# A DLRM tower on one core: the first two one-hot fields made as a couple, and the half grams of tiles 2 and 3 placed around the layers of tiles 0 to 2

## The reference, cut to what matters

```
e = stack([tbl_f[ids[:, f]] for f in 26 fields])     # (512, 26, 128)
T = concat([dense, e])                               # (512, 27, 128)
Z = einsum('bnd,bmd->bnm', T, T); z = Z[upper triangle]   # 351 numbers per sample
h = relu(concat([z, dense]) @ W_top1 + b_top1)       # 479 -> 512
h = relu(h @ W_top2 + b_top2)                        # 512 -> 256
y = h @ W_top3                                       # 256 -> 1
```

## Time and profile before

| what | value |
|---|---|
| median of 3 runs (lowest to highest) | 122.86 us (122.41 to 123.29) |
| the profiled execution's own time | 122.26 us |
| its span, first to last instruction | 120.5 us |
| TensorE busy (matmul) | 110.3 us, 92% |
| VectorE busy | 86.0 us, 71% |
| ScalarE busy | 80.3 us, 67% |
| GpSimd busy | 61.9 us, 51% |
| last one-hot matmul starts | 71.08 us |

### The profile page before, as it was taken

One profiled execution on the slowest core, in us unless ns is written; L12 is line 12 of the kernel. 1 busy time (PEld: TensorE's weight loads), 2 busy tenths in 40 slices (PEclk: granted clock), 3 DMA queues, 4 the chain that ended last, 5 costly groups with the idle time before them and its releaser, 6 DMA issues.

```text
span 120.5 us, 2624 instructions
## 1 busy us (share of the span) xinstructions
PE 110.3 (92%) x1008; PEld 92.0 (76%) x1008; DVE 86.0 (71%) x180; ACT 80.3 (67%) x150; POOL 61.9 (51%) x60
## 2 busy tenths in 40 slices
PE   5999799999999999999999975997989899859993
PEld 5967577688678888887787855996979689859990
DVE  5689999988789699787987621699722459875141
ACT  4479981977999999999976851787930029793011
POOL 7578777777777787877778674000600000022000
DMA  2999559999999269961111122000110000101000
GB/s 68 310 365 397 218 159 367 392 400 380 398 356 365 82 220 409 373 165 33 34 44 44 44 54 60 0 5 20 27 42 0 0 5 0 27 4 23 5 0 1
DMA packets 7638, 17.75 MB, mean 147 GB/s; under 512 B 1965, under 2 KB 2889, under 8 KB 7497
## 3 DMA queue, kind: packets, MB, share of 16 engines
q1 hardware_dynamic: 5770, 14.13, 31.9%
q0 software_dynamic: 1632, 3.19, 9.0%
q10 hardware_dynamic: 222, 0.26, 0.7%
HBM read 17.33 MB, written 0.00 MB: 144 GB/s over the span
## 4 chain that ended last, share of the span: by engine, by line
PE 63%; DMA 11%; DVE 9%; issue 5%; ACT 5%; SPq 5%; ACTq 0%; DVEq 0%
PE work L469 20%; PE work L471 19%; PE work L417 8%; DMA table<-small 8%; PE work L526 5%; DMA Zt<-table 4%; PE work L427 4%; SPq L328 3%; DVE hot L734 3%; PE tp L453 3%; DVE t_lo L703 2%; PE work L536 1%; DVE Zt L568 1%; ACT Zt L568 1%; ACT table L560 1%
## 5 line engine op out<-in xcount | busy, mean ns | idle before, releaser
L400 POOL DMA_INDIRECT rows<-tbl,idx x48 | 58.1, 1211 | 25.8 <-issue 12.8
L469 PE MATMUL work<-hot,t_hi 128*128 128x512 f32 x128 | 52.2, 407 | 1.1 <-DVE hot L734 0.7
L471 PE MATMUL work<-hot,t_lo 128*128 128x512 f32 x128 | 50.4, 394 | 0.0
L734 DVE TENSOR_SCALAR hot<-ids_bc,rownum 128x1024 fp32r<-128x1024 int32 (+1 forms) x59 | 38.7, 697 | 6.7 <-PE work L471 4.9
L469 PEld LDWEIGHTS work<-hot,t_hi 128*128 128x128 f32 x128 | 24.4, 190 | 10.2 <-DVE hot L734 2.5
L471 PEld LDWEIGHTS work<-hot,t_lo 128*128 128x128 f32 x128 | 24.4, 190 | 4.3
L588 ACT CAST t_hi<-table 128x1280 fp32r<-128x1280 f32 (+3 forms) x16 | 16.8, 1050 | 5.8 <-DMA table<-small 5.3
L703 DVE TENSOR_TENSOR t_lo<-table,t_hi 128x1280 fp32r<-128x1280 f32 (+3 forms) x16 | 19.5, 1220 | 1.4 <-DVE minus_row L695 1.0
L427 PE MATMUL work<-XT 128*58 128x52 f32 x512 | 15.8, 217 | 2.7 <-issue 2.1
L427 PEld LDWEIGHTS work<-XT 128*58 128x58 f32 x512 | 14.7, 133 | 4.3 <-issue 4.1
L560 ACT COPY table<-work 14x224 f32<-14x224 f32 x16 | 5.7, 355 | 13.9 <-PE work L427 13.1
(11 more groups left out here) (47 smaller groups left out, 59.2 us busy)
## 6 DMA issues: line engine op xcount, KB each, us to landing
table<-small SPq DMA_DIRECT2D x8, 640.0 KB
ids_bc<-ids_oh SPq DMA_DIRECT2D x6, 512.0 KB, 3.3
table<-small SPq DMA_DIRECT2D x4, 512.0 KB
w_sb<-w SPq DMA_DIRECT2D x1, 1024.0 KB
rows<-tbl,idx POOLq DMA_INDIRECT x48
table<-small SPq DMA_DIRECT2D x2, 320.0 KB
ids_bc<-ids_oh SPq DMA_DIRECT2D x2, 256.0 KB, 3.4
w_sb<-w SPq DMA_DIRECT2D x1, 512.0 KB
```

Source lines behind the costliest of these rows:

```text
L400: nc.gpsimd.indirect_dma_start(rows[:, t, place - FIRST, :], None, tbls[f], bass.IndirectOffsetOnAxis(ap=idx[:, t, place - FIRST:place - F ...
L469: nc.tensor.matmul(bank, t_hi[:, i % PARTS, c * D:(c + 1) * D], hot[:, k % HOTS, :], start=row_chunk(i, c) == 0, stop=False)
L471: last = nc.tensor.matmul(bank, t_lo[:, i % PARTS, c * D:(c + 1) * D], hot[:, k % HOTS, :], start=False, stop=row_chunk(i, c) == n - 1)
L734: nc.vector.tensor_scalar(hot[:, k % HOTS:k % HOTS + n, :], ids_bc[:, ids_slot(f):ids_slot(f) + n, :], rownum[:, v, at:at + 1], None, ALU. ...
```

## The change

The first two fields become a couple like the others. `SINGLES` goes; the couple's chunks alternate, and only the first chunk of each of the two fields keeps a 512-wide one-hot (`LONE = 2`); the others are 1024 wide. ScalarE makes the last couple of tables 0 and 1. The second table comes as one DMA (`HEADED = 1`), the ids of field 1 come right behind those of field 0, and the ids of fields 4 and 5 have slots of their own, so nothing waits for them. The low parts for the first two tables stand at other one-hots. The rows steps (2, 1) and (2, 2) move from the tail into the one-hot phase (after tables 11 and 12), both copied by ScalarE. In the tail `dense` of tile 0 goes first, and the halves come earlier, the layers later. The PSUM bank of each field shifts by 4, so that the bank of layer 1 is free early. Gathers 44 and 45 now wait for the fifth half, 46 and 47 for the sixth (before: 46 and 47 for the fourth).

```diff
-VECTOR_ROWS = [(2, 1), (3, 1)]
+VECTOR_ROWS = [(3, 1)]
-HEADED = 2
+HEADED = 1
-SINGLES = 2
+LONE = 2
-GATHER_AFTER = {46: ("gram", 4)}
-ACT_EVERY = 5
-ACT_TABLES = [3, 5, 6, 7, 8, 9, 10, 11, 12, 13]
+GATHER_AFTER = {44: ("gram", 5), 46: ("gram", 6)}
+ACT_TABLES = [0, 1, 3, 5, 6, 7, 8, 9, 10, 11, 12, 13]
-ROWS_AFTER = {..., 9: [(1, 2)], 11: [(2, 0)]}
+ROWS_AFTER = {..., 9: [(1, 2)], 10: [(2, 0)], 11: [(2, 1)], 12: [(2, 2)]}

-LOW_PARTS = {(i, 5 if i < SINGLES else 4 if OH_CHUNKS[i] == 8 else 6): (i + 1, 0, OH_CHUNKS[i + 1])
-             for i in range(1, K_OH - 1)}
-LOW_PARTS.update({(0, 0): (0, 0, HEAD), (0, 4): (0, HEAD, OH_CHUNKS[0]), (0, 5): (1, 0, HEAD),
-                  (1, 1): (1, HEAD, OH_CHUNKS[1])})
+LOW_PARTS = {(i, 4 if OH_CHUNKS[i] == 8 else 6): (i + 1, 0, OH_CHUNKS[i + 1]) for i in range(K_OH - 1)}
+LOW_PARTS.update({(0, 0): (0, 0, HEAD), (0, 2): (0, HEAD, OH_CHUNKS[0])})

-    steps += [("burst", 0, 0), ("gram", 0, 0), ("rows", 2, 1), ("burst", 0, 1), ("gram", 0, 1),
-              ("rows", 2, 2), ("dense", 0, 0), ("burst", 1, 0), ("gram", 1, 0), ("burst", 1, 1),
-              ("gram", 1, 1), ("layer1", 0, 0), ("layer1", 0, 1), ("rows", 3, 0), ("layer2", 0, 0), ("dense", 1, 0),
-              ("layer1", 1, 0), ("layer1", 1, 1), ("rows", 3, 1), ("layer2", 1, 0), ("burst", 2, 0), ("gram", 2, 0),
-              ("rows", 3, 2), ("burst", 2, 1), ("gram", 2, 1), ("dense", 2, 0), ("burst", 3, 0),
-              ("gram", 3, 0), ("burst", 3, 1), ("gram", 3, 1), ("layer1", 2, 0), ("layer1", 2, 1), ("dense", 3, 0),
-              ("layer2", 2, 0), ("layer1", 3, 0), ("layer2", 3, 0), ("turn", 0, 0), ("layer3", 3, 0)]
+    steps += [("dense", 0, 0), ("burst", 0, 0), ("gram", 0, 0), ("burst", 0, 1), ("gram", 0, 1), ("rows", 3, 0),
+              ("burst", 1, 0), ("gram", 1, 0), ("rows", 3, 1), ("burst", 1, 1), ("gram", 1, 1), ("burst", 2, 0),
+              ("gram", 2, 0), ("layer1", 0, 0), ("layer1", 0, 1), ("burst", 2, 1), ("gram", 2, 1), ("dense", 1, 0),
+              ("layer2", 0, 0), ("layer1", 1, 0), ("layer1", 1, 1), ("rows", 3, 2), ("burst", 3, 0), ("gram", 3, 0),
+              ("dense", 2, 0), ("layer2", 1, 0), ("burst", 3, 1), ("gram", 3, 1), ("layer1", 2, 0), ("layer1", 2, 1),
+              ("dense", 3, 0), ("layer2", 2, 0), ("layer1", 3, 0), ("layer2", 3, 0), ("turn", 0, 0), ("layer3", 3, 0)]

-    return i if i < SINGLES else i - (i - SINGLES) % 2          # pair_of
+    return i - i % 2
-    return f if f < SINGLES else (f - SINGLES + IDS - 2) % IDS  # ids_slot
+    return f % IDS
-            return work[:, (i - K_OH) % LOOKUP_BANKS, :]
+            return work[:, (i - K_OH + GRAM_BANKS) % LOOKUP_BANKS, :]

             def table_ids(i):
-                if i >= SINGLES + 2:
-                    sp.wait_ge(hot_used, groups_used(first_hot(ids_free(i))))
+                if i >= IDS:
+                    sp.wait_ge(hot_used, groups_used(first_hot(i - IDS + 2)))
-            table_ids(0)
+            for f in range(LONE):
+                sp.dma_start(ids_bc[:, f, :], ids_oh[f, :, :]).then_inc(ids_in[f], 16)

             # ScalarE, ahead of the steps and in them
             high_part(0, 0, HEAD)
+            high_part(0, HEAD, OH_CHUNKS[0])
             distance(0)
-            high_part(0, HEAD, OH_CHUNKS[0])
-            one_hot(mine_in(0)[0])
-            high_part(1, 0, HEAD)
-            distance(1)
-            high_part(1, HEAD, OH_CHUNKS[1])
+            high_part(1, 0, OH_CHUNKS[1])
...
+                    if 1 < i < K_OH - 2:
                         high_part(i + 2, 0, OH_CHUNKS[i + 2])
+                    for m in mine_in(i):
+                        one_hot(m)
+                        if i == 0:
+                            distance(1)
+                    if i <= 1:
+                        high_part(i + 2, 0, OH_CHUNKS[i + 2])
+                    if i > 1:
                         copy_lookups(i - 2)
```

More of the change, by code:

```diff
@@ L57 @@
 CHUNKS_BEHIND = 14
-GATHER_AFTER = {46: ("gram", 4)}
-ACT_EVERY = 5
-ACT_TABLES = [3, 5, 6, 7, 8, 9, 10, 11, 12, 13]
+GATHER_AFTER = {44: ("gram", 5), 46: ("gram", 6)}
+ACT_TABLES = [0, 1, 3, 5, 6, 7, 8, 9, 10, 11, 12, 13]
 DENSE_AFTER = 5
 COPIED_AFTER = 8
-ROWS_AFTER = {4: [(0, 0)], 5: [(0, 1)], 6: [(0, 2)], 7: [(1, 0)], 8: [(1, 1)], 9: [(1, 2)], 11: [(2, 0)]}
+ROWS_AFTER = {4: [(0, 0)], 5: [(0, 1)], 6: [(0, 2)], 7: [(1, 0)], 8: [(1, 1)], 9: [(1, 2)], 10: [(2, 0)], 11: [(2, 1)],
+              12: [(2, 2)]}
 GATHERED = [f for f in range(FIELDS) if f not in ONEHOT]
@@ L174, in pair_of @@
 def pair_of(i):
-    return i if i < SINGLES else i - (i - SINGLES) % 2
+    return i - i % 2
 def field_of(i, c):
-    return i if i < SINGLES else pair_of(i) + c % 2
+    return pair_of(i) + c % 2
 def row_chunk(i, c):
-    return c if i < SINGLES else (i - pair_of(i)) * OH_CHUNKS[i] // 2 + c // 2
+    return i % 2 * OH_CHUNKS[i] // 2 + c // 2
 def looked_up(f):
-    return first_hot(f + 1 if f < SINGLES else pair_of(f) + 2)
+    return first_hot(pair_of(f) + 2)
 def ids_slot(f):
-    return f if f < SINGLES else (f - SINGLES + IDS - 2) % IDS
-def ids_free(f):
-    return max(2, f - IDS + 2)
+    return f % IDS
 TABLE_OF = [i for i in range(K_OH) for _ in range(OH_CHUNKS[i])]
-HOT_FIRST = [k for k, i in enumerate(TABLE_OF) if i < SINGLES or (k - first_hot(i)) % 2 == 0]
+HOT_FIRST = [k for k in range(len(TABLE_OF)) if k < LONE or k % 2 == 0]
 def hot_width(m):
-    return 1 if TABLE_OF[HOT_FIRST[m]] < SINGLES else 2
+    return 1 if HOT_FIRST[m] < LONE else 2
 def by_scalar(m):
     i = TABLE_OF[HOT_FIRST[m]]
-    if i < SINGLES:
-        return m % ACT_EVERY == ACT_EVERY - 1
     return i in ACT_TABLES and HOT_FIRST[m] + 2 == first_hot(i + 1)
@@ L333, in table_ids @@
             def table_ids(i):
-                n = 1 if i < SINGLES else 2
-                if i >= SINGLES + 2:
-                    sp.wait_ge(hot_used, groups_used(first_hot(ids_free(i))))
-                sp.dma_start(ids_bc[:, ids_slot(i):ids_slot(i) + n, :],
-                             ids_oh[i:i + n, :, :].rearrange("f p b -> p f b")).then_inc(ids_in[i], 16)
+                if i >= IDS:
+                    sp.wait_ge(hot_used, groups_used(first_hot(i - IDS + 2)))
+                sp.dma_start(ids_bc[:, ids_slot(i):ids_slot(i) + 2, :],
+                             ids_oh[i:i + 2, :, :].rearrange("f p b -> p f b")).then_inc(ids_in[i], 16)
             sp.dma_start(idx[:], ids.rearrange("p (t f) -> p t f", t=TILES)).then_inc(idx_in, 16)
-            table_ids(0)
+            for f in range(LONE):
+                sp.dma_start(ids_bc[:, f, :], ids_oh[f, :, :]).then_inc(ids_in[f], 16)
             for i in range(K_OH):
@@ L482, in _ @@
                         pe.wait_ge(xt_ready, 1)
+                    elif halves == 1:
+                        pe.wait_ge(lookup_copied, K_OH - 1)
+                        pe.wait_ge(lookup_dve, 2)
                     if halves >= HALVES:
@@ L491, in _ @@
                     if t == 0:
-                        pe.wait_ge(lookup_copied, K_OH - 1)
-                        pe.wait_ge(lookup_dve, 2)
                         pe.wait_ge(w1_in, 16)
@@ L601, in distance @@
                 act.wait_ge(ids_in[f], 16)
+                if f == 0:
+                    act.wait_ge(ids_in[1], 16)
                 act.wait_ge(rownum_ready, 2)
@@ L633, in _ @@
             high_part(0, 0, HEAD)
+            high_part(0, HEAD, OH_CHUNKS[0])
             distance(0)
-            high_part(0, HEAD, OH_CHUNKS[0])
-            one_hot(mine_in(0)[0])
-            high_part(1, 0, HEAD)
-            distance(1)
-            high_part(1, HEAD, OH_CHUNKS[1])
+            high_part(1, 0, OH_CHUNKS[1])
             for kind, t, i in STEPS:
                 if kind == "onehot":
[L642 to L647, removed]
-                        high_part(i + 2, 0, OH_CHUNKS[i + 2])
[L649 to L654, removed]
+                    if 1 < i < K_OH - 2:
+                        high_part(i + 2, 0, OH_CHUNKS[i + 2])
+                    for m in mine_in(i):
[5 more added lines that the diff above has]
+                    if i > 1:
                         copy_lookups(i - 2)
@@ L724, in _ @@
                     dve.wait_ge(ids_in[f], 16)
-                    n = 1 if i < SINGLES else 2
-                    for c in range(0, OH_CHUNKS[i], n):
+                    for c in range(OH_CHUNKS[i]):
                         if (i, c) in LOW_PARTS and i + c:
@@ L729, in _ @@
                         k = first_hot(i) + c
[L730 to L736, removed]
+                        if k not in HOT_FIRST or by_scalar(HOT_FIRST.index(k)):
+                            continue
+                        n = hot_width(HOT_FIRST.index(k))
+                        if k == 1:
+                            dve.wait_ge(ids_in[1], 16)
+                        if k >= HOTS:
+                            dve.wait_ge(hot_used, groups_used(k + n - HOTS))
```

(12 more changed lines are left out.)

## The result

The changed kernel takes 124.96 us (median, 124.37 to 125.22) against 122.63 for the kernel before (four runs: the three of its median and one more, 120.81 to 123.29); the ratio is 1.029, 95% interval 1.025 to 1.034. It is slower, where the forecast was 122.8 us with a range up to 124.7. The profiled execution took 124.37 us, span 122.5. The ratios are of the faster runs of both kernels (they leave out nine of the 19 runs of before beside E1 to E4, more than 1.5% above the fastest), so they can differ from the quotient of the medians, which take all runs.

A forecast was written before the change was run, and what follows sets the result against it. TensorE holds 63% of the wait chain: VectorE, ScalarE and DMA feed it at the start, order decides the tail. +2.1 - 1.05 - 0.15 - 0.9 + 0 = 0.0 on 122.26 profiled; 122.8 us against the median, range 120.9 to 124.7.

The forecast's parts named there:

- The feeding of the start: One-hot start: late casts and low parts idle TensorE about 1.8 us before chunk 2, 1.5 before chunk 4; chunk 13 +2.1 us.
- From 11.8 it is fed ... Chunk 13 starts at 11.8 + 9 x 0.456 + 0.1 = 16.0: One-hot start: from chunk 4 TensorE runs unstarved at 0.456 us a chunk; chunk 13 at 16.0 instead of 13.91, +2.1 us.
- my second rival: Start: idle stops drop TensorE's clock, 0.4 us more per chunk for some six chunks, +2.4 us, 125.2 us; chance 0.13.
- Up to chunk 46: One-hot phase: earlier tables return 1.4 us of lost time but for a 0.35 us stall at chunk 46; -1.05 us.
- Rows moved: Two groups of transposes leave the tail for the one-hot phase, at 0.46 us each there; -0.1 to -0.2 us.
- dense: Start of the tail: dense of tile 0 fills TensorE's 0.81 us wait for the last lookups; -0.9 us.
- The tail's idle time: Tail: 3.4 us of new waits for copies and a relu against 3.4 us of old waits that go; 0 net.
- 1.6 + 0.3 + 0.1 + 0.95 + 0.45: Tail waits: half (2, 0), half (1, 0), half (1, 1), rows (3, 2) before half (3, 0), last relu; sum 3.4 us.
- The 0.95: Tail: idle us beyond its own 0.58 at rows step (3, 2), directly ahead of half (3, 0), which needs its copy.
- The stall in the first half: Tail: 1.33 us of TensorE idle inside the first half, no releaser named, kept; bounds 0 and twice as much.
- The expected gain of the couple: Start: VectorE's 13 one-hots of 512 become 2 of 512 and 5 of 1024; costed at nothing, TensorE being slower behind chunk 4.

The follow-up runs named there:

- E1: The changed kernel with unread transposes on TensorE, 22 ahead of chunk 2 and 8 ahead of chunk 4: 122.31 us, ratio to before 1.009.
- E4: The new start alone, with the tail order, rows and banks of the kernel before: 125.10 us, ratio to before 1.028.
- E2: The changed kernel with 16 unread transposes on TensorE ahead of half (2, 0) in the tail: 123.45 us.
- E5: The kernel before, profiled again with no edit: 122.09 us, span 120.3.
- E3: The new tail order, moved rows and shifted banks, with the start of the kernel before: 120.58 us, ratio to before 0.990.
- E6: The changed kernel with two low parts (table 0's tail, table 1) moved behind later one-hots on VectorE: 121.05 us, ratio to before 0.989.
- E7: The changed kernel with field 1's ids behind the tail of table 0 in SyncE's queue: 124.25 us, no interval.
- E11: The tail-only kernel of E3 with 16 unread transposes ahead of half (2, 0), order kept: 120.28 us.

## Why the prediction was wrong, point by point

- **The feeding of the start** was worked out nearly right: chunk 4 at 11.8, measured 12.03. Chunk 2 was expected at 9.3 and came at 9.64, because the table's tail landed 0.3 us later than a bandwidth of 351 KB per us gave. The stop ahead of chunk 2 was a full 2.80 us where the prediction had 1.8: the first two chunks were also done earlier, the fast level having come at about 6.0 instead of 7.2 us.
- **The step that failed** is "From 11.8 it is fed ... Chunk 13 starts at 11.8 + 9 x 0.456 + 0.1 = 16.0": it prices the chunks at the fast level. Chunks 4 to 8 ran at 1.2 GHz, and chunk 13 came at 18.14. That was my second rival, at +2.4 us and 0.13. Its mechanism is the one that happened in every run of the changed kernel; E1 puts the price at 1.9 us, and the nine chunks from chunk 4 on took 2.3 and 2.6 us more than E1's in the profiles of E4 and E2. That its 125.2 us came within 0.3 us of the median is in part luck: it had neither the tail's fall nor the stall that went away. My argument against it was that 0.8 us of idle at 71.47 had not brought long matmuls back. That row was too short to speak against 2.80 us, more than three times as long; I had written myself that no row had such a stretch. The rule that I quoted from the Trainium skill ("TensorE: Matmul & The Clock Gate", What's actually happening), that the throttled clock is the default and activity releases it, agrees with the trace now: the granted clock is 0.50 behind the stop, and the matmuls are back at 0.23 us apart from 16.3 on, after 6.7 us of work with one short stop.
- **Up to chunk 46**: -1.05 forecast. From chunk 13 to 46 it was 16.0 us against 16.9 before, -0.9, and the stall ahead of chunk 46 is there. Right.
- **Rows moved** -0.1 to -0.2, **dense** -0.9: the last one-hot is 0.9 us further behind for the two groups, and the first half starts 1.22 us after the last matmul's start, as before (1.20), with dense inside. Right.
- **The tail's idle time**: forecast 1.6 + 0.3 + 0.1 + 0.95 + 0.45; measured 2.15, 0.43, none, 0.80, 0.33, in sum 3.7 against 3.4. (The 0.95 doesn't follow from its rows: 61.75 to 63.12 is 1.37, less 0.58 is 0.79, which is what was measured.) The largest is 0.55 short. ScalarE's copies of a tile's second half took 3.56 us (80.97 to 84.53), because the row at 84.53 starts only when its two DMA issues have ended at 84.49, and the first of them took 1.28 us. I had taken 3.0 us from tile 2 of the kernel before, where that issue took 0.69. Tile 0 of the same trace has 3.58 us:

```profile
78.48 0.71 ACT L560 COPY table<-work 14x224 f32<-14x224 f32 x2
80.01 1.24 ACTq L328 DMA_DIRECT2D Zt<-table  x1
82.06 0.72 ACT L576 COPY XT<-tp 128x512 f32<-128x512 f32 x1 [1.21 <-issue]
```

Why the first issue is longer for tile 0 is not shown. The step's other omission is the greater: I asked the clock question of the start alone. The same idle stretch in the tail dropped the clock and made half (2, 0) 1.5 us longer (E2).
- **The stall in the first half**, kept at 1.33 us: it was absent in the changed kernel and in the kernel before profiled again (E5), and E4's first half took 2.15 us in one piece. One execution's rows without a releaser were taken as a property. Its absence offset most of the second fall.

In sum, from the forecast 122.26 on the profiled time: +1.9 for the clock at the start, +0.2 for the later table, +1.5 for the clock in the tail, +0.3 for waits, -1.3 for the stall gives 124.9; the profiled execution took 124.37, so half a microsecond stays unexplained.

The expected gain of the couple, less work on VectorE, was rightly put at nothing: busy time there fell from 86.0 to 84.2 us.

## What to carry to other kernels

When a change opens an idle stretch on TensorE, price the work behind it at both clock levels, and look in every stage, not only where the first one is; here a wait of 2.2 us was followed by a fall in four of E3's ten runs, while all twelve runs of the changed kernel, E2 and E4, whose stops at the start were 2.3 to 3.3 us in the profiles, read a granted clock under 1.000. A row in which a shorter stop did no harm is no evidence about a longer one. Where copies bound a run of like blocks, one block that needs no copy, put between them, is worth more than a closer packing; and a low part or cast that is not needed yet must not stand in front of a one-hot that is. A stage's gain or loss read from one trace of each kernel can be off by more than a microsecond: here two traces of the kernel before put the last one-hot matmul 1.5 us apart.

## What the runs showed of the hardware that I had not expected

- TensorE's clock is not a matter of the kernel alone. After the same wait of 2.15 to 2.18 us in the tail, the half took 1.92 us in E1, 2.07 in E6, 3.09 in E3, 3.44 in the changed kernel and 3.45 in E7; E3's ten runs split six to four by granted clock, with medians 120.3 and 122.1 us. The kernel before is not free of it either: five of its 37 runs beside E1 to E11 read 0.986 and took 124.2 to 126.5 us, and the others, at 1.000, spread from 120.7 to 123.9.
- The granted clock read 1.00 over 5 to 10 us in the kernel before, while its matmuls up to 7 us were the long ones; in the changed kernel the column shows the falls near 10 and near 88 us. The matmuls' own spacing is the safer reading.
- Unread transposes cost nothing that these runs show where they lie in a wait, and the level stayed fast: in E2 the half still waited 0.30 us for ScalarE behind 16 of them, and E1 is 2.65 us faster than the same kernel without them.
- DMA issues in ScalarE's list hold its next copy: two of 1.28 and 0.75 us, ending at 84.49, in front of the copy at 84.53.
